# GpSimd adds the output bias to the next batch's x in four pieces, one step earlier in its queue

## The reference

```
x = x + tanh(g_xattn) * (attention(layernorm(x), ctx, ctx) @ W_o.T + b_o)
x = x + tanh(g_ffn)   * experts(layernorm(x))
```

## Time and profile before

| | us |
|---|---|
| median of three runs | 341.07 |
| lowest, highest | 340.63, 341.73 |
| the profiled execution's own time | 339.78 |
| its span, from the first instruction to the last | 338.0 |
| attention, up to the first expert product | about 180 |

### The profile page before, as it was taken

The page is one execution under the profiler, slowest core; times in us unless marked ns, Lnnn a source line. Parts: engine busy times, 40 slices in busy tenths (PEclk is TensorE's granted clock), DMA queues, the critical chain, the costliest instruction groups (busy, mean ns, idle before and its releaser), DMA issues.

```text
span 338.0 us, 8493 instructions
## 1 busy us (share of the span) xinstructions
PE 311.0 (92%) x2823; PEld 249.8 (74%) x2823; DVE 205.1 (61%) x980; ACT 172.9 (51%) x651; POOL 149.6 (44%) x181
## 2 busy tenths in 40 slices
PE   8868979999999899988889999999999999999990
PEld 4536846876688675767668888888888988888870
DVE  2799788999999988999972423333222333233320
ACT  2489999998999899999222111111111111111110
POOL 6389566776697746666453122111222222211122
PEclk9998999999999999999999999999999999999996
DMA  7811595119121831203054898899888888888400
GB/s 217 290 58 24 182 375 164 26 37 334 37 95 57 230 117 62 88 22 95 5 186 145 257 317 263 283 299 289 271 275 260 277 277 275 258 269 277 139 18 12
DMA packets 42070, 60.54 MB, mean 179 GB/s; under 512 B 3704, under 2 KB 32912, under 8 KB 42032
## 3 DMA queue, kind: packets, MB, share of 16 engines
q1 hardware_dynamic: 38928, 53.28, 50.1%
q0 software_dynamic: 2560, 6.25, 5.3%
q10 hardware_dynamic: 544, 0.52, 0.4%
HBM read 44.60 MB, written 14.19 MB: 174 GB/s over the span
## 4 chain that ended last, share of the span: by engine, by line
PE 62%; ACT 16%; DVE 13%; issue 5%; POOL 1%; DVEq 0%; POOLq 0%; ACTq 0%
PE bank L1637 21%; PE bank L1654 17%; ACT probs L649 12%; PE bank L1665 5%; DVE probs L850 3%; PE bank L1269 3%; PE bank L1322 3%; DVE rows L925 2%; PE bank L1280 2%; ACT q_par L623 2%; PE bank L1230 2%; PE bank L1310 2%; ACT probsT L662 2%; PE bank L1620 1%; DVE probsT L869 1%
## 5 line engine op out<-in xcount | busy, mean ns | idle before, releaser
L649 ACT ACTIVATE probs<-probs,low 128x128 f32<-128x128 f32 x256 | 99.2, 402 | 2.3 <-DVE low L850 2.3
L780 ACT ACTIVATE w_raw<-bank 128x480 f32<-128x480 f32 (+1 forms) x48 | 25.3, 527 | 122.0 <-PE bank L1637 122.0
L492 POOL TENSOR_TENSOR probs<-probs,r_total 128x512 f32<-128x512 f32 x64 | 66.3, 1049 | 29.5 <-DVE r_total L859 29.2
L1637 PE MATMUL bank<-xdT,w 128*128 128x160 f32 x512 | 75.1, 300 | 0.2 <-DVE xdT L1185 0.2
L1637 PEld LDWEIGHTS bank<-xdT,w 128*128 128x128 f32 x512 | 71.6, 190 | 1.5 <-issue 0.7
L580 POOL DMA_INDIRECT out_dram<-base,place x16 | 14.0, 878 | 115.9 <-DVE base L1206 115.9
L1654 PE MATMUL bank<-w,w_raw 128*128 128x256 f32 x256 | 62.4, 386 | 0.0
L850 DVE CUSTOM_DVE_ANT_0 probs<-bank,mask_now 128x128 f32<-128x128 f32 x256 | 57.2, 282 | 3.9 <-PE bank L1310 3.3
L1198 DVE SCALAR_TENSOR_TENSOR base<-bank,base 32x256 f32<-32x256 f32 x64 | 30.6, 478 | 47.0 <-PE bank L1665 45.3
L1654 PEld LDWEIGHTS bank<-w,w_raw 128*128 128x128 f32 x256 | 46.4, 190 | 11.5 <-issue 6.6
L649 ACT ACTIVATION_READ_ACCUMULATOR probs<-probs,low 128x1 f32 x256 | 51.8, 202 | 0.0
(11 more groups left out here) (123 smaller groups left out, 417.1 us busy)
## 6 DMA issues: line engine op xcount, KB each, us to landing
w<-in_L_ffn_w_dram SPq DMA_DIRECT2D x32, 1024.0 KB, 6.2
expert_queue<-empty_row SPq DMA_DIRECT2D x1, 5140.0 KB, 18.2
q_rows<-expert_queue SPq DMA_DIRECT2D x16, 160.0 KB, 6.1
base<-expert_queue SPq DMA_DIRECT2D x16, 129.0 KB, 5.6
ctx_rows<-in_ctx_dram SPq DMA_DIRECT2D x4, 512.0 KB, 9.1
out_dram<-rows SPq DMA_DIRECT2D x4, 512.0 KB, 7.2
x_all<-in_x_dram SPq DMA_DIRECT2D x3, 512.0 KB, 7.2
v_shift<-v SPq DMA_DIRECT2D x12, 128.0 KB, 2.3
```

The lines of the kernel that those rows point to most:

```text
L492: pool.tensor_tensor(probs[:, i % NP_], probs[:, i % NP_], r_total[:, i % NP_].unsqueeze(2).to_broadcast([P, PAIRS, 2 * WINDOW]), ALU.mult ...
L649: last = act.activation(probs[:, i % NP_, j], probs[:, i % NP_, j], ACT.Exp, scale=-1.0, bias=low[:, i % NP_, j:j + 1], accum_out=total[:, ...
L780: act.activation(hidden[:, ms[0]:ms[-1] + 1, :], ps_hidden[m][:, 0:n].rearrange("p (m c) -> p m c", c=CAP), ACT.Gelu_apprx_tanh).then_inc( ...
L1637: last = pe.matmul(ps_hidden[m][:, c * CAP:(c + 1) * CAP], w1_sb[i % 2][:, k, f * P:(f + 1) * P], xdT[i % 2][:, k], start=(k == 0), stop=( ...
```

## The change

```diff
                 pool.wait_ge(xn_ready, value(n, 1, 1))
                 pool.wait_ge(bias_ready, 2)
-                pool.tensor_tensor(x_all[:, n], x_all[:, n], bias_og[:].unsqueeze(1).to_broadcast([P, T, D]),
-                                   ALU.add).then_inc(x_based, 1)
+                for t in range(T):
+                    last = pool.tensor_tensor(x_all[:, n, t], x_all[:, n, t], bias_og[:], ALU.add)
+                last.then_inc(x_based, 1)
...
                 norm(b, 5)
+                base_of(b + 1)
                 x1_rstd_of(b - 1, 1)
                 norm(b, 6)
-                base_of(b + 1)
                 norm(b, 7)
```

## The result

The change is slower: 345.04 us median (343.68 to 345.23, 6 runs) against 341.4 of the kernel before in the same comparison (340.63 to 341.82, 6 runs), a ratio of 1.0109 (95% interval 1.0093 to 1.0124), 3.6 us. 340.3 was forecast, within 339.4 to 341.7. The profiled execution of after took 344.42 us, its span 342.6, at a granted clock of 0.982. Lines from L485 on are one or more higher than before.

A forecast was written before the change was run, and what follows sets the result against it. PE is busy 92% of the span, but around the change the chain of waits runs through DVE's x1_norm, delayed by POOL, then PE. -1.30 + 0.55 = -0.75 us takes 341.07 to 340.3, range 339.4 to 341.7.

The forecast's parts named there:

- The addition leaves its old place: Second half's x1_norm, batches 1 and 2: it meets only norm 8; PE's waits of 0.63 and 0.67 us go, 1.30 less.
- The cost of a piece: POOL's idle time behind norm 5: each piece takes 0.62 us, 2.5 in all, fitting a hole of 2.39 with cover.
- What the pieces meet there: First half's x1_norm: its second instruction waits for one piece, 0.28 and 0.27 us late, 0.55 more for two batches.
- DVE waits for all four pieces: Rival, first half's x1_norm: POOL keeps its hold until the last piece; 3.0 us more, 344.1; chance 0.08.
- The third case: x1_norm instruction at 104.27, batch 2: ended 0.17 us behind norm 5, taken to agree with the rule of about 0.16.
- rival I: Follow-up rival, batch 2: the length of POOL's unbroken run decides, whatever it holds; pair about 3.8 us, ratio near 1.011.
- Theory D: Follow-up theory: POOL's cores drift apart over back-to-back instructions, denying DVE its turn; a wait realigns them, pair 1.5 to 1.9 us.
- Batch 0: base_of(0) up to 0.8 us later, base_of(1) ending near 35.4 instead of 32.90, with 4.7 us of cover: no cost.

The follow-up runs named there:

- Version 4: Kernel before, with the whole addition in one instruction behind norm 8, POOL first waiting for the second half's x1_norm: 340.3 us, ratio 0.9959.
- Version 9: The changed kernel, with POOL waiting for the first half's x1_norm of the batch before ahead of the four pieces: 340.31 us, ratio 0.9982 against the kernel before.
- 2: Kernel before, with the whole addition as one instruction in the new place, behind norm 5: 346.88 us, ratio 1.0169.
- 6: Four pieces everywhere, in the new place only in batch 2, in the old place otherwise: 344.46 us, ratio 1.0099 against the kernel before.
- 7: The changed kernel with the last batch's mask work (cast and two products) left out: 343.26 us, ratio 1.0073 against the kernel before.
- 17: The changed kernel; in batch 2 a product of 648 numbers replaces the second scatter, which comes later: 344.87 us, ratio 1.0111 against the kernel before.
- 18: The changed kernel; in batch 2 a memset of 16 numbers added behind the second scatter: 345.43 us, ratio 1.0101 against the kernel before.
- 3: The changed kernel with a semaphore wait between the pieces, each waiting for the one before: 342.83 us, ratio 1.0036 against the kernel before.
- 14: The changed kernel; in batch 2 a product of 512 numbers replaces the second scatter, which comes later: 340.26 us, ratio 1.0008 against the kernel before.
- 10: The changed kernel, with POOL waiting for norm 5's own end ahead of the four pieces: 341.68 us, ratio 1.0021 against the kernel before.
- 13: The changed kernel; in batch 2 POOL waits for the end of norm 3 before norm 4: 340.55 us, ratio 1.0027 against the kernel before.
- 1: Four pieces in the old place, behind norm 6, against the kernel before: 340.49 us, ratio 0.9984.
- the probes: Kernel before with groups added at its end: POOL runs products, then four pieces, while DVE asks; in all 49 groups DVE's first instruction ended about 0.15 us behind the last product.
- 16: Kernel before with 24 groups of products and four pieces added at its end, every second with an indirect DMA directly ahead; DVE got in each time; no kernel time given.
- 8: Kernel before with the last batch's mask work (cast and two products) left out: 340.65 us, ratio 0.9992.
- 11: Kernel before with the addition of the bias left out for batches 1 to 3: 339.53 us, ratio 0.9957.

## Why the prediction was wrong, point by point

**The addition leaves its old place: right.** The second half's pair fell to 1.10 in both batches, norm 8 stood by itself, and PE's waits of 0.63 and 0.67 us went. Version 4, which has this and nothing in the new place, shows it in a time: 1.4 us by its ratio, where 1.30 was forecast. Version 9 gains 0.6 us, within its uncertainty, with the loss at the router in it.

**The cost of a piece: a little low.** 0.62 was taken, with 0.59 and 0.79 as ends; the median was 0.73 (0.71 to 0.78), 2.76 to 2.88 for four. It was taken from the mask's product, which works on bf16 and not on the same kind of operands, and from it I had read that there was no fixed cost to be seen. They still fit the hole, and the deviations were not late.

**What the pieces meet there: this step failed.** It said that DVE gets its turn at the next boundary, so only its second instruction waits, for one piece, 0.28 us in each batch. In batch 1 that is what came: 0.41 us, the 0.28 and a piece longer by 0.11, and PE 0.28 us earlier in all. In batch 2 the first instruction waited for all four, +2.73 us on DVE where 0.27 stood in the sum. That is the rival "DVE waits for all four pieces", at 0.08, in one of the two batches. That its price for both batches, 344.1, lies near the measured 345.04 is chance: only one batch paid it, and the router paid the rest. With what was measured the sum would have been -1.30 + 0.41 + 2.73 + 1.05 = +2.9 us, where the medians say +3.6. I had generalised from the earlier trace rows: both boundaries at which DVE was seen to get in, norm 7 to norm 8, lie some 5.3 us behind a wait of POOL of 2.4 us (69.96 to 75.26 in batch 1). The third case, 104.27, was no evidence, as nothing stood behind norm 5 there. In batch 2 of after POOL's last longer idle time ended at 93.16, 13 us before the pieces. Between lay gaps of 0.17 us ahead of its DMAs and one wait of 0.08 us, of the deviations' second instruction for the first (97.96), 8.3 us before the pieces.

What the runs show of the cause: in batch 2 DVE was passed over in each kernel in which the three norms ran with no wait between them up to the pieces or the addition (after, 2, 6, 7, 17, 18, and 3 up to its first inner wait), and in none in which POOL had waited there, be it 0.06 us (14), 0.11 (10, counted in the same way) or 0.13 (13). So a wait of POOL close ahead gives DVE its turn back; 10 shows it with everything up to norm 5's end as in after. That a DMA directly ahead is needed is refuted by 17; whether one further back plays a part is not shown. The moment of asking alone doesn't decide: in batch 2 0.51 to 0.63 us before the next start was passed over and 0.35, 0.69 and 0.72 was not, but DVE got in at 0.63 in batch 1 of after (its second instruction), at 0.42, 0.47 and 0.94 in 1, and at 0.41 to 1.05 in the probes.

One thing does order all the profiles: the time from POOL's last wait on a semaphore to the start at which DVE could have got in, if the gaps at a DMA are not counted as waits. At the seven places where DVE was passed over it was 8.2 to 8.3 us (106.23 - 97.96 in after), and where it got in it was at most 6.5. The longest of these are 5.8 and 6.5 us in 16 (four products behind a DMA) (counted from the start of the group, a memset at 445.25 in the rows above) and 5.5 in 1, whose POOL and DVE in batch 2 are these:

```profile
107.35 0.72 POOL L460 TENSOR_TENSOR rstd<-var_eps,minus_half 128x2 f32<-128x2 f32 x1
...
111.81 2.13 POOL L493 TENSOR_TENSOR probs<-probs,r_total 128x512 f32<-128x512 f32 x2
```

```profile
111.35 1.70 DVE L926 TENSOR_SCALAR rows<-rows,mean_var,rstd 128x256 f32<-128x256 f32 x2
```

This is rival I, the length of the run, with the addition that a wait of 0.06 us ends a run. The seven places have the same instructions of POOL before them, but for one replaced (17) or added (18), and the length was never varied alone, so why a long run loses DVE its turn, and at what length, stays open. Theory D, with a drift that needs longer than 6.5 us, is not excluded.

**Not on the list: the router of batch 1, +1.05 us.** The term was missing altogether. The wanted gain moved the router by more than the mask's cast, and onto it (7 and 8 show the cost; it comes with no addition at all, 11, and stays away in 4). By this the new place, mended, is worth only the 0.6 us of version 9, within its uncertainty. Version 15 tried to move the mask's work one unit later in version 9:

```diff
-                mask_of(b + 2)
                 norm(b, 12)
+                mask_of(b + 2)
```

> The change, with GpSimd waiting for the first half's x1_norm before the pieces (the version that gave a ratio of 0.998 with a pair of 0.79 and 1.08 but lost about 1 us at the router of batch 1), and the mask's cast and products one unit later, behind norm 12. Theory (two-input VectorE instructions of the router, marks and onehot, are stretched when they meet the mask's work, and this costs the 1.0 us): onehot back at about 0.26 and marks at about 0.29 in batch 1, time 0.7 to 1.3 us under before, ratio about 0.997. Rival (the mask's work only meets other instructions of VectorE one unit later, or norm 12 keeps its place and nothing moves): ratio 0.998 to 1.001, and marks or others show over 0.6.

Measured: 340.1 us (339.02 to 341.59), 1.0001 (0.9982 to 1.0021). `marks` and `onehot` are back at 0.23, and the profiled execution's span is 337.3, but the runs spread over 2.6 us, the expected 0.997 did not come, and no gain can be told: inconclusive.

**Batch 0: right.** The four pieces of `base_of(1)` ended at 35.12 (35.4 forecast) and nobody waited.

## What to carry to other kernels

Before work is put on GpSimd ahead of or beside VectorE instructions that exclude it, ask how long GpSimd has been running without a wait at that place: up to 6.5 us behind a wait VectorE got in at the next boundary, in a backlog of 8.2 us it stood behind everything that was ready. If the order matters, write it as a wait (version 9, version 4) and don't leave it to who is first. Version 4, behind the VectorE instructions, is the only one that gained time. And when an engine is made earlier by a microsecond, go through the short two-input instructions behind it for a new meeting with GpSimd, as 0.17 us cost 1.05 here.

## What the runs showed that was not expected

- A wait of GpSimd of about 0.1 us decides over 2 us and more of VectorE's time: directly ahead of the pieces (10: pair 1.56 instead of 3.80), and also 2 us ahead of them (13: 1.64). In 14 it was 0.06 us.
- A GpSimd addition of 256 numbers takes 0.71 to 0.75 us when nobody gets in, 0.76 to 0.78 when VectorE does without a wait of GpSimd: a hint in the trace of who got the turn. The pieces follow each other every 0.68 to 0.69 us; in before norm 7 starts 2.32 us behind the start of the addition of 1024. So a piece has an estimated 0.14 us of fixed cost ((4 x 0.685 - 2.32) / 3).
- 3.10 us of idleness of TensorE were followed by a granted clock of 0.50 for over 2 us in one profiled execution (6); in four others, with 3.04 to 3.17 us (after, 7, 17, 18), it stayed at 1.00.
